# Third batch's output projection beside the sixteenth attention group instead of the fourteenth

## The chip, the cores and the metric

One core of one Trainium2 chip runs the whole kernel. The metric is the device time of one execution in microseconds (us); the engines are PE (TensorE, with PEld its weight loads), DVE (VectorE), ACT (ScalarE), POOL (GpSimd) and SP (SyncE, which here only issues DMAs).

## The reference

A gated cross-attention block and a gated mixture-of-experts block, in float32. Cut to what matters:

```python
# x (4, 512, 512); ctx (4, 1601, 512); 16 heads of 32
q = rms_norm(linear(layernorm(x), q_w, q_b), norm_q_w)
k, v          = ... of ctx[:, 257:]     # 1344 text rows
k_img, v_img  = ... of ctx[:, :257]     # 257 image rows
out = attention(q, k, v) + attention(q, k_img, v_img)   # softmax(q k^T / sqrt(32)) v
x = x + tanh(g_xattn[0]) * linear(out, o_w, o_b)
x = x + tanh(g_ffn[0]) * ffn(layernorm(x))              # shared expert and the top 2 of 8 experts
```

## The kernel before

**Stages.** The program projects queries, keys and values and writes them to DRAM, then runs the attention, then the feed-forward part. The change lies in the attention, which ends about 1269 us into the span. Semaphores alone order the engines; each engine's program is written out by hand.

**Groups and steps.** The attention has 16 groups `G` of 4 heads of one batch: batch `b` is groups 4b to 4b+3 (counted from 0, so the fourteenth group is G=13 and the sixteenth G=15). A group has 13 steps `kt`, one for each 128 of the 1601 keys. In a step PE makes four score products (`score`, L954), ACT takes their exponentials into one of four `P` buffers (`exps`, L1079), PE multiplies an earlier step's `P` with the values (`weigh`, L909), and POOL adds the `P` of steps 1 to 7 into `sacc` (`add`, L1261); DVE adds that of step 8 (L1203), after which `sacc` is complete (`d_add`). The exponentials of step kt wait until step kt-4's `P` has been both weighed and added, so ACT runs at most four steps ahead of POOL. Scores go to three PSUM banks, so PE is at most three score products ahead of ACT.

**Work of the next group.** Beside its own steps, each group but the last makes 64 small products for the softmax maxima of the next group (`units`, L439 on PE, L632 on DVE), 7 of them in step 0. They need the next group's keys, whose DMAs SP issues at step 10 of the group before. G=15 has no such products.

**Results.** A group's result `oi` is split into a high part `aTh` (ACT, L1097) and a low part `aTl` (POOL, L1278), two groups later at step 1. When the four groups of a batch are there, `pe_project_tile` multiplies them with the output weight: 4 tiles of 12 matmuls (L49, L50, L51), one tile after the scores of steps 4, 6, 8 and 10 of groups 5, 9 and 13. `dve_project_tile` adds each tile to `acc` (L1136) and takes its mean and variance (L1138, L1140). The fourth batch's 4 tiles stand behind the last group, where DVE and ACT finish its result in quarters (L1233 to L1243, L1129).

**Also in the last group.** At steps 2, 5 and 8 SP loads the first feed-forward weights into dead value buffers (L894); at steps 4, 7 and 10 ACT rounds them (L1122) and DVE takes the rest (L1219). SP waits for the earlier piece before it issues the next one. Every group also clears a 2 MB piece of `Xg` by DMA (L896), as SP's step 5.

Of the kernel before, what the change touches and what calls it, by code (L numbers as in the profile page):

```python
# [6 lines left out]
F32 = mybir.dt.float32  # L7
F32R = mybir.dt.float32r
U32 = mybir.dt.uint32
ACT = mybir.ActivationFunctionType  # L10
ALU = mybir.AluOpType
AX = mybir.AxisListType

NB = 4
# [10 lines left out]
NG = 4 * NB  # L25
# [13 lines left out]
def program(nc, ap, ctx):  # L39
    pe, dve, act, pool, sp = nc.tensor, nc.vector, nc.scalar, nc.gpsimd, nc.sync  # L40
# [7 lines left out]
    def mm3(out, ah, al, bh, bl, first, last):  # L48
        pe.matmul(out, ah, bh, start=first, stop=False)  # L49
        pe.matmul(out, ah, bl, start=False, stop=False)  # L50
        return pe.matmul(out, al, bh, start=False, stop=last)  # L51
# [160 lines left out]
    def rows_ra(G):  # L212


        return 64 + 65 * G + 4 * sum(x < G for x in (5, 9, 13))

    def head_rows(d, G, c0, c1):
        return d[128 * (G % 4):128 * (G % 4) + 128, c0:c1].rearrange("(j p) s -> p j s", p=32)
# [619 lines left out]
    BANKS_RA = (0, 1, 5)  # L838
# [7 lines left out]
    def exp_no(G, kt, j):  # L846
        return 52 * G + 4 * kt + j + 1
# [12 lines left out]
    def sum_no(G, kt):  # L860
        return 7 * G + max(1, kt)

    def slot(G, kt):
        return (NKT * G + kt) % 4

# [6 lines left out]
    def sp_attend():  # L872
        all_projected(sp)
        sp.dma_start(wo[:], ap["o_wT"].rearrange("(k p) o -> p k o", p=128)).then_inc(s_wo, 16)
        load_queries(2)
        load_values(1)
        for step in range(NSTEP):
            G, kt = divmod(step, NKT)
            pG = G - 1
            if kt == 12 and G + 1 < NG:  # L880
                store_mrow(G + 1)
            if kt == 1 and G >= 1 and pG + 2 < NG:
                sp.wait_ge(p_pv, pv_no(pG, 12))
                load_values(pG + 2)
            for i in range(3):
                if step == LASTG + 2 + 3 * i:
                    if i == 0:
                        sp.wait_ge(p_pv, pv_no(NG - 2, 12))
                        sp.wait_ge(p_sc, exp_no(NG - 2, 12, 3))
                    else:  # L890
                        sp.wait_ge(a_early, i)
                        sp.wait_ge(d_early, i)
                    for q in range(2):
                        sp.dma_start(early[:, :, 256 * q:256 * q + 256], first_weights(2 * i, q)).then_inc(s_gu, 16)  # L894
            if kt == 5 and G < NG:
                sp.dma_start(Xg[1024 * G:1024 * G + 1024, :], ap["zeros"]).then_inc(s_zero, 16)  # L896
            if kt == 10 and G + 2 < NG:
                sp.wait_ge(p_sc, exp_no(G, 9, 3))
                load_keys(G + 2, 0)
            if kt == 12 and G + 2 < NG:  # L900
                sp.wait_ge(p_sc, exp_no(G, 12, 3))
                load_keys(G + 2, 1)
                if G + 3 < NG:
                    load_queries(G + 3)
# [4 lines left out]
            ins = pe.matmul(ps[32 * j:32 * j + 32, bank, :], w(j), pt[p0:p1_, j, :], start=first, stop=last, tile_position=(p0, 32 * j))  # L909
        return ins  # L910

    def pe_project_tile(t, bank):
        for kk in range(4):
            ins = mm3(ps[:, bank, :], aTh[:, kk, 128 * t:128 * t + 128], aTl[:, kk, 128 * t:128 * t + 128],
                      Woh[:, kk, :], Wol[:, kk, :], kk == 0, kk == 3)
        ins.then_inc(p_ra, 1)

    def pe_attend():
# [3 lines left out]
        def ra_bank():  # L922
            if ra >= 68:
                pe.wait_ge(d_ra, ra - 2)
            return BANKS_RA[(ra - 65) % 3]
# [67 lines left out]
        for step in range(NSTEP):  # L993
            G, kt = divmod(step, NKT)
            more = G + 1 < NG
            plan = PLAN[kt] if more else [0] * 7
            at = sum(map(sum, PLAN[:kt])) if more else 0
            upto = [at + sum(plan[:i]) for i in range(8)]

            def place(i):  # L1000
                units(G + 1, upto[i], plan[i])

            def scored(j):
                if G < NG:
                    score(G, kt, j)

            if kt == 0:
                place(0)
                place(1)
                if G:  # L1010
                    image(G - 1)
                place(2)
                for j in range(4):
                    scored(j)
                    place(3 + j)
                continue
            scored(0)
            place(0)
            scored(1)
            place(1)  # L1020
            if kt == 1 and G:
                image_end(G - 1)
            if kt == 3:
                weigh(G, 0, 0, 128, True, False)
            if 3 <= kt < 11:
                weigh(G, kt - 2, 0, 128, False, False)
            if kt == 11:
                text_end(G)
            if kt == 12:
                weigh(G, 10, 64, 128, True, False)  # L1030
                if more:
                    pe.wait_ge(d_mx, G + 2)
                    pe.wait_ge(d_ra, ra)
                    pe_mrow(BANKS_RA[(ra - 65) % 3])
                    ra += 1
            place(2)
            scored(2)
            place(3)
            scored(3)
            place(4)  # L1040
            place(5)
            place(6)
            if G in (5, 9, 13) and kt in (4, 6, 8, 10):
                if kt == 4:
                    pe.wait_ge(a_ath, G - 1)
                    pe.wait_ge(g_atl, G - 1)
                    if G == 5:
                        pe.wait_ge(g_wol, 4)
                pe_project_tile((kt - 4) // 2, ra_bank())
                ra += 1  # L1050
        for t in range(4):
            pe.wait_ge(a_ath, NG + t)
            pe.wait_ge(d_last, 7 * t + 7)
            pe_project_tile(t, ra_bank())
            ra += 1


# [5 lines left out]
    def act_attend():  # L1063
# [27 lines left out]
        def split(G):  # L1091
            if G == 0:
                act.wait_ge(g_wol, 4)
            act.wait_ge(g_oi, 2 * G + 2)
            if G >= 4 and G % 4 == 0:
                act.wait_ge(p_ra, rows_ra(G + 2) + 1)
            act.activation(aTh[:, G % 4, :], oi[:], ACT.Copy).then_inc(a_ath, 1)  # L1097

        for step in range(NSTEP):
            G, kt = divmod(step, NKT)  # L1100
# [25 lines left out]
        for t in range(4):  # L1126
            cs = slice(128 * t, 128 * t + 128)
            act.wait_ge(d_last, 7 * t + 6)
            act.activation(aTh[:, 3, cs], oi[:, cs], ACT.Copy).then_inc(a_ath, 1)  # L1129
        root_of_variance_act(NB - 1)  # L1130


    def dve_project_tile(b, t, ra, bank):
        k = 4 * b + t
        dve.wait_ge(p_ra, ra + 1)
        dve.scalar_tensor_tensor(acc[:, k, :], ps[:, bank, :], tg[:, 0:1], acc[:, k, :], ALU.mult, ALU.add).then_inc(d_ra, 1)  # L1136
        dve.wait_ge(d_ra, ra + 1)
        dve.bn_stats(st3[:, k, 0:6], acc[:, k, :]).then_inc(d_st3, 1)  # L1138
        dve.wait_ge(d_st3, 2 * k + 1)
        dve.bn_aggr(st3[:, k, 6:8], st3[:, k, 0:6]).then_inc(d_st3, 1)  # L1140
# [8 lines left out]
    def dve_attend():  # L1149
# [17 lines left out]
        for step in range(NSTEP):  # L1167
# [41 lines left out]
                reciprocals(pG, (2,))  # L1209
            else:  # L1210
                units(G + 1, at, sum(plan))
            if G in (5, 9, 13) and kt in (4, 6, 8, 10):
                dve_project_tile((G - 5) // 4, (kt - 4) // 2, ra, BANKS_RA[(ra - 65) % 3])
                ra += 1
            for i in range(3):
                if step == LASTG + 4 + 3 * i:
# [14 lines left out]
        for t in range(4):  # L1231
            cs = slice(128 * t, 128 * t + 128)
            dve.tensor_tensor(oi[:, cs], ps[:, 6, cs], rt[:, cs], ALU.mult).then_inc(d_last, 1)  # L1233
            dve.wait_ge(d_last, 7 * t + 1)
            dve.tensor_tensor(rt[:, cs], rt[:, cs], ps[:, 7, cs], ALU.mult).then_inc(d_last, 1)
            dve.tensor_tensor(ot[:, cs], ot[:, cs], ps[:, 7, cs], ALU.mult).then_inc(d_last, 1)
            dve.wait_ge(d_last, 7 * t + 3)
            dve.reciprocal(rt[:, cs], rt[:, cs]).then_inc(d_last, 1)
            dve.tensor_tensor(oi[:, cs], oi[:, cs], ot[:, cs], ALU.add).then_inc(d_last, 1)
            dve.wait_ge(d_last, 7 * t + 5)  # L1240
            dve.tensor_tensor(oi[:, cs], oi[:, cs], rt[:, cs], ALU.mult).then_inc(d_last, 1)
            dve.wait_ge(a_ath, NG + t)
            dve.tensor_tensor(aTl[:, 3, cs], oi[:, cs], aTh[:, 3, cs].bitcast(F32), ALU.subtract).then_inc(d_last, 1)  # L1243
            if t:
                dve_project_tile(NB - 1, t - 1, ra, BANKS_RA[(ra - 65) % 3])
                ra += 1
# [4 lines left out]
    def pool_attend():  # L1251
# [21 lines left out]

        def split(G):
            pool.wait_ge(a_ath, G + 1)
            if G >= 4 and G % 4 == 0:
                pool.wait_ge(p_ra, rows_ra(G + 2) + 1)
            pool.tensor_tensor(aTl[:, G % 4, :], oi[:], aTh[:, G % 4, :].bitcast(F32), ALU.subtract).then_inc(g_atl, 1)  # L1278

        for step in range(NSTEP):  # L1280
            G, kt = divmod(step, NKT)
# [838 lines left out]
```

## Time and profile before

| | |
|---|---|
| median of 3 runs | 1810.65 us (1809.1 to 1810.71) |
| profiled execution | 1810.86 us, its span 1809.5 us |
| busy share of the span | PE 96%, DVE 66%, POOL 52%, ACT 45% |
| a group that follows a plain group | 49.96 us (G=8, most of the others) |
| groups 5, 9 and 13, with tiles | 62.19, 62.27 and 64.88 us |

A group's length is read between two starts of the one ACT instruction L638 that each group has at its step 12 (for example at 1075.05 and 1139.93 us for G=13). In the profile, busy time of PE holds matmuls that overlap in the array, so that 96% does not say that it never waits; the granted clock (PEclk) is 1.00 at 2.4 GHz and 0.50 at 1.2 GHz.

### The profile page before, as it was taken

Reading aid. Unit: us, or ns where it says so; the run is one execution under the profiler, and the core shown is the slowest. Engines: PE = TensorE matmul, PEld = TensorE weight load, DVE = VectorE, ACT = ScalarE, POOL = GpSimd, SP = SyncE. Lnnn points to the kernel's source line nnn. Section 1 sums busy time; section 2 is a strip of 40 time slices with the busy share of each in tenths; the row PEclk is TensorE's granted clock in tenths of the full one; section 3 lists DMA queues with packets and bytes.
Section 4 is the critical chain, followed back from the end, with each engine's and each line's share of the span. In section 5 each row is a group of like instructions: output and inputs, shape, how many; then the busy total and the mean of one; then the engine's idle time right before and its main releaser. Section 6 shows DMA issues by size and latency. Waiting matters only on the chain. (4 is left out here: it accounts for less than half of the span.)

```text
span 1809.5 us, 24750 instructions
## 1 busy us (share of the span) xinstructions
PE 1737.9 (96%) x8822; PEld 1119.7 (62%) x8822; DVE 1190.3 (66%) x2242; ACT 820.1 (45%) x1519; POOL 940.5 (52%) x323
## 2 busy tenths in 40 slices
PE   5999999999999999999999999997899999999999
PEld 4888878874444445444444445433676778878777
DVE  5776777667887777888778777835555445443555
ACT  4443332336555554565556554563221265554221
POOL 3221311118776664777746667673242377776442
PEclk8999999999999999999999999998999999999999
DMA  9456759546544553454355433320221578887442
GB/s 315 124 173 200 228 173 231 173 149 165 136 116 118 138 138 66 122 133 124 108 138 138 115 92 89 102 71 12 97 104 49 174 227 262 272 277 230 147 121 93
DMA packets 185234, 268.73 MB, mean 149 GB/s; under 512 B 24956, under 2 KB 121996, under 8 KB 184596
## 3 DMA queue, kind: packets, MB, share of 16 engines
q1 hardware_dynamic: 179992, 250.36, 47.6%
q0 software_dynamic: 5120, 16.78, 2.7%
q8 instruction: 71, 1.16, 0.3%
q14 instruction: 51, 0.42, 0.1%
HBM read 194.10 MB, written 105.93 MB: 166 GB/s over the span
## 5 line engine op out<-in xcount | busy, mean ns | idle before, releaser
L1079 ACT ACTIVATE P<-ps 128x512 f32<-128x512 f32 (+1 forms) x832 | 442.6, 597 | 330.9 <-PE ps L954 276.0
L632 DVE TENSOR_REDUCE mp<-ps 128x1 f32<-128x448 f32 x768 | 428.2, 615 | 96.0 <-PE ps L439 95.4
L1261 POOL TENSOR_TENSOR sacc<-sacc,P 128x2048 f32<-128x2048 f32 x96 | 441.6, 4600 | 13.8
L439 PE MATMUL ps<-Kst,Qst 96*128 96x448 f32 (+1 forms) x1024 | 386.9, 392 | 12.1 <-DMA Kst<-KLd 6.2
L954 PE MATMUL ps<-Qst,Kst 100*128 100x512 f32 (+1 forms) x832 | 323.5, 409 | 10.4 <-ACT P L1079 10.0
L439 PEld LDWEIGHTS ps<-Kst,Qst 96*128 96x128 f32 x1024 | 191.6, 188 | 227.9 <-DVE mp L632 141.3
L909 PE MATMUL ps<-P,Vg 128*32 128x512 f32 (+2 forms) x1792 | 237.8, 612 | 0.0
L808 POOL TENSOR_TENSOR cl<-craw,ch 128x1024 fp32r<-128x1024 f32 (+2 forms) x26 | 61.9, 2380 | 288.3 <-ACT ch L544 288.3
L954 PEld LDWEIGHTS ps<-Qst,Kst 100*128 100x128 f32 (+1 forms) x832 | 152.7, 186 | 69.9 <-ACT P L1079 43.4
L49 PE MATMUL ps<-W,ch 128*128 128x512 f32 (+1 forms) x408 | 162.7, 399 | 0.0
L51 PE MATMUL ps<-W,cl 128*128 128x512 f32 (+1 forms) x408 | 159.7, 392 | 0.0
L50 PE MATMUL ps<-W,ch 128*128 128x512 f32 (+1 forms) x408 | 159.6, 391 | 0.0
L2019 POOL TENSOR_TENSOR gul<-gur,guh 128x2048 fp32r<-128x2048 f32 x15 | 69.4, 4629 | 115.5 <-ACT guh L1692 115.4
L632 DVE TENSOR_REDUCE mx<-ps 128x1 f32<-128x258 f32 x256 | 96.0, 420 | 30.9 <-PE ps L439 30.3
L1261 POOL TENSOR_TENSOR sacc<-P 128x2048 f32<-128x2048 f32 x16 | 73.3, 4583 | 63.8 <-ACT P L1079 38.6
L2019 POOL TENSOR_TENSOR Kst<-gur,Kst 128x2048 fp32r<-128x2048 f32 x15 | 69.4, 4626 | 44.5 <-ACT Kst L1692 44.5
L51 PEld LDWEIGHTS ps<-W,cl 128*128 128x128 f32 (+1 forms) x408 | 75.9, 186 | 17.9 <-issue 0.2
L49 PEld LDWEIGHTS ps<-W,ch 128*128 128x128 f32 (+1 forms) x408 | 76.2, 187 | 15.4 <-issue 0.2
L50 PEld LDWEIGHTS ps<-W,ch 128*128 128x128 f32 (+1 forms) x408 | 76.2, 187 | 15.3
L909 PEld LDWEIGHTS ps<-P,Vg 128*32 128x32 f32 (+2 forms) x1792 | 39.0, 108 | 72.9 <-issue 44.3
L909 PE MATMUL ps<-P,ones 64*32 64x512 f32 (+2 forms) x640 | 82.7, 602 | 0.0
L564 ACT ACTIVATE junk<-kf 128x512 f32<-128x512 f32 (+1 forms) x51 | 32.2, 631 | 108.6 <-DVE kf L680 108.6
(227 smaller groups left out, 3008.2 us busy)
## 6 DMA issues: line engine op xcount, KB each, us to landing
gur<-in_w_gate_up SPq DMA_DIRECT2D x23, 1024.0 KB, 8.1
Kst<-KHd SPq DMA_DIRECT2D x32, 640.0 KB, 8.1
Vd<-vf SPq DMA_DIRECT2D x50, 256.0 KB, 2.3
craw<-in_ctxT SPq DMA_DIRECT2D x24, 512.0 KB, 4.7
KHd<-sth SPq DMA_DIRECT2D x24, 512.0 KB, 3.5
KLd<-stl SPq DMA_DIRECT2D x24, 512.0 KB, 4.7
dnr<-in_w_down SPq DMA_DIRECT2D x23, 512.0 KB, 3.9
xg<-Xg SPq DMA_DIRECT2D x23, 512.0 KB, 8.2
```

Of the source, the lines that this page charges most:

```text
L49: pe.matmul(out, ah, bh, start=first, stop=False)
L50: pe.matmul(out, ah, bl, start=False, stop=False)
L51: return pe.matmul(out, al, bh, start=False, stop=last)
L439: pe.matmul(ps[:, bank, 0:c1 - c0], Qst[G % 3][0:96, j, 128 * qt:128 * qt + 128], Kst[G % 2][0:96, j, c0:c1], start=True, stop=True).then_ ...
L564: act.activation(junk[:rows], kf[:rows, u % 3, :], ACT.Square, accum_out=stk[:rows, u % 4, 0:1]).then_inc(a_sqk, 1)
L632: dve.reduce_max(out, ps[:, bank, 0:c1 - c0], AX.X).then_inc(d_ra, 1)
L808: pool.tensor_tensor(cl[:, n % 3, :, 0:c1 - c0], craw[:, n % 3, :, 0:c1 - c0], ch[:, n % 2, :, 0:c1 - c0].bitcast(F32), ALU.subtract).then ...
L909: ins = pe.matmul(ps[32 * j:32 * j + 32, bank, :], w(j), pt[p0:p1_, j, :], start=first, stop=last, tile_position=(p0, 32 * j))
L954: pe.matmul(ps[:m, 2 + (e - 1) % 3, :], Kst[s][0:100, j, 128 * kt:128 * kt + m], Qst[G % 3][0:100, j, :], start=True, stop=True).then_inc( ...
L1079: act.activation(P[slot(G, kt)][:m, j, :], ps[:m, 2 + (e - 1) % 3, :], ACT.Exp, scale=SCALE).then_inc(a_exp, 1)
L1261: pool.tensor_tensor(sacc[:], (P[slot(G, 0)] if kt == 1 else sacc)[:], P[slot(G, kt)][:], ALU.add).then_inc(g_sum, 1)
L2019: pool.tensor_tensor(gul[q % 2], gur[raw_slot(q)][:], guh[q % 2].bitcast(F32), ALU.subtract).then_inc(g_gu, 1)
```

## The change

The third batch's four tiles leave steps 4, 6, 8 and 10 of group 13 and stand at the same steps of group 15. Since `aTh` and `aTl` must then hold the third batch longer, the results of groups 12 to 15 go to the query buffers `Qst[1]` and `Qst[2]` once the last group that reads them is through (`a_high`, `a_low`). The waits follow. The clearing DMA of `Xg` moves from step 5 to step 2 in SP's program.

```diff
-        return 64 + 65 * G + 4 * sum(x < G for x in (5, 9, 13))
+        return 64 + 65 * G + 4 * sum(x < G for x in (5, 9))
...
+    PROJECTED = {5: 0, 9: 1, 15: 2}
+
+    def a_high(G):
+
+        return aTh[:, G % 4, :] if G < 12 else Qst[1 if G < 14 else 2][:, 2 * (G % 2), :]
+
+    def a_low(G):
+        return aTl[:, G % 4, :] if G < 12 else Qst[1 if G < 14 else 2][:, 2 * (G % 2) + 1, :]
...
-            if kt == 5 and G < NG:
+            if kt == 2 and G < NG:
                 sp.dma_start(Xg[1024 * G:1024 * G + 1024, :], ap["zeros"]).then_inc(s_zero, 16)
...
-            if G in (5, 9, 13) and kt in (4, 6, 8, 10):
+            if G in PROJECTED and kt in (4, 6, 8, 10):
+                b = PROJECTED[G]
                 if kt == 4:
-                    pe.wait_ge(a_ath, G - 1)
-                    pe.wait_ge(g_atl, G - 1)
-                    if G == 5:
+                    pe.wait_ge(a_ath, 4 * b + 4)
+                    pe.wait_ge(g_atl, 4 * b + 4)
+                    if b == 0:
                         pe.wait_ge(g_wol, 4)
-                pe_project_tile((kt - 4) // 2, ra_bank())
+                pe_project_tile(b, (kt - 4) // 2, ra_bank())
                 ra += 1
...
-            if G >= 4 and G % 4 == 0:
+            if G in (4, 8):
                 act.wait_ge(p_ra, rows_ra(G + 2) + 1)
-            act.activation(aTh[:, G % 4, :], oi[:], ACT.Copy).then_inc(a_ath, 1)
+            if G >= 12:
+                act.wait_ge(p_sc, exp_no(13 if G < 14 else 14, 12, 3))
+            act.activation(a_high(G), oi[:], ACT.Copy).then_inc(a_ath, 1)
...
-            if G in (5, 9, 13) and kt in (4, 6, 8, 10):
-                dve_project_tile((G - 5) // 4, (kt - 4) // 2, ra, BANKS_RA[(ra - 65) % 3])
+            if G in PROJECTED and kt in (4, 6, 8, 10):
+                dve_project_tile(PROJECTED[G], (kt - 4) // 2, ra, BANKS_RA[(ra - 65) % 3])
                 ra += 1
```

POOL's `split` and the last four tiles change in the same way. Line numbers in the order of the change are higher by 9 to 16 than those of the profile (L954 is L964 there, L909 L919, L1136 L1149, L1219 L1232, L1165 L1178, L1203 L1216).

PE, last group, from step 9's late scores to the start of step 11's end; before:

```order
L954 MATMUL ps<-Qst,Kst 128x512 x4
L909 MATMUL ps<-P,Vg 32x512 x4
L954 MATMUL ps<-Qst,Kst 128x512 x4
L909 MATMUL ps<-P,Vg 32x512 x8
L909 MATMUL ps<-P,ones 32x512 x8
L954 MATMUL ps<-Qst,Kst 128x512 x2
```

PE, the same place in the change:

```order
L964 MATMUL ps<-Qst,Kst 128x512 x4
L919 MATMUL ps<-P,Vg 32x512 x4
L964 MATMUL ps<-Qst,Kst 128x512 x2
L49 MATMUL ps<-Woh,aTh 128x512
L50 MATMUL ps<-Wol,aTh 128x512
L51 MATMUL ps<-Woh,aTl 128x512
...
L964 MATMUL ps<-Qst,Kst 128x512 x2
L919 MATMUL ps<-P,Vg 32x512 x8
L919 MATMUL ps<-P,ones 32x512 x8
L964 MATMUL ps<-Qst,Kst 128x512 x2
```

The fourth tile (12 matmuls, of which three are shown) now stands between step 10's last score and step 11's first, ahead of the eight value products and eight row sums that close the text part.

DVE, last group, from the third early weight to the end of the `sacc` sum; before:

```order
L1219 TENSOR_TENSOR Kst<-Vg,Kst 128x1024 x3
L1165 RECIPROCAL rt<-rt 128x128
L1203 TENSOR_TENSOR sacc<-sacc,P 128x2048
L1165 RECIPROCAL rt<-rt 128x128 x3
```

DVE, the same place in the change:

```order
L1149 SCALAR_TENSOR_TENSOR acc<-ps,tg,acc 128x512
L1151 BN_STATS st<-acc 128x6
L1153 BN_AGGR st<-st 128x2
L1232 TENSOR_TENSOR Kst<-Vg,Kst 128x1024
L1178 RECIPROCAL rt<-rt 128x128
L1216 TENSOR_TENSOR sacc<-sacc,P 128x2048
L1178 RECIPROCAL rt<-rt 128x128 x3
```

The three instructions of the fourth tile, which wait for PE's tile, stand ahead of the third early weight and of the addition that completes `sacc`.

SP, from the last group's two row copies on; before:

```order
L321 DMA Qst<-mrh 2x4x512
L321 DMA Qst<-mrl 2x4x512
L894 DMA Vg<-in_w_sh_gate_up 128x2x256 x4
L896 DMA Xg<-in_zeros 32x16384
L894 DMA Vg<-in_w_sh_down 128x2x256 x2
```

SP, the same place in the change:

```order
L321 DMA Qst<-mrh 2x4x512
L321 DMA Qst<-mrl 2x4x512
L904 DMA Vg<-in_w_sh_gate_up 128x2x256 x2
L906 DMA Xg<-in_zeros 32x16384
L904 DMA Vg<-in_w_sh_gate_up 128x2x256 x2
L904 DMA Vg<-in_w_sh_down 128x2x256 x2
```

Only here does the clearing DMA pass anything: it now goes out behind the first early weight instead of behind the second. In the groups before, it follows the value loads either way.

## Rows read from the trace of the kernel before

**Rows 1.** Windows of six groups: length; busy PE, PEld, DVE, ACT, POOL; PEclk; DMA.

```profile
548.61:601.35 52.74, 50.72 (x281) 23.08 (x280) 40.47 (x74) 29.61 (x56) 35.89 (x10) 0.97 0.45 118
651.74:713.93 62.19, 61.33 (x329) 31.64 (x328) 46.13 (x86) 29.90 (x56) 35.97 (x10) 1.00 0.40 101
713.93:763.28 49.35, 48.83 (x281) 22.93 (x280) 40.32 (x74) 29.59 (x56) 35.96 (x10) 1.00 0.50 126
813.24:863.20 49.96, 49.07 (x281) 22.84 (x280) 40.30 (x74) 29.65 (x56) 35.90 (x10) 1.00 0.49 125
1075.05:1139.93 64.88, 62.87 (x329) 31.82 (x328) 46.29 (x86) 29.90 (x56) 35.97 (x10) 0.97 0.38 96
1139.93:1189.53 49.60, 49.10 (x281) 22.72 (x280) 40.30 (x74) 29.64 (x56) 35.92 (x10) 1.00 0.23 71
```

**Rows 2.** PE's timeline where groups 3 and 13 begin: start, length, instruction, [idle before].

```profile
550.54 0.68 PE L439 MATMUL ps<-Kst,Qst 96*128 96x448 f32 x2 [1.51 <-DMA Kst<-KLd]
...
1076.84 0.84 PE L439 MATMUL ps<-Kst,Qst 96*128 96x448 f32 x2 [1.36 <-DMA Kst<-KLd]
```

**Rows 3.** Windows of 5 us: start of group 13, and two in group 15.

```profile
1075.00:1080.00 5.00, 3.63 (x17) 0.90 (x18) 3.55 (x5) 1.93 (x4) 0.49 (x1) 0.72 0.18 39
...
1209.00:1214.00 5.00, 4.78 (x24) 1.74 (x24) 1.44 (x1) 4.23 (x9) 4.86 (x2) 1.00 0.45 144
...
1219.00:1224.00 5.00, 3.46 (x11) 1.07 (x11) 1.89 (x1) 2.08 (x4) 4.86 (x2) 0.66 0.38 121
```

**Rows 4.** PE's timeline, group 13: first matmul of its fourth tile, and the next score.

```profile
1129.12 0.50 PE L49 MATMUL ps<-Woh,aTh 128*128 128x512 f32 x1
...
1131.97 0.40 PE L954 MATMUL ps<-Qst,Kst 100*128 100x512 f32 x1
```

**Rows 5.** POOL's timeline, group 15: its additions of steps 1 to 7.

```profile
1200.32 4.57 POOL L1261 TENSOR_TENSOR sacc<-P 128x2048 f32<-128x2048 f32 x1 [1.68 <-ACT P L1079]
1205.03 29.62 POOL L1261 TENSOR_TENSOR sacc<-sacc,P 128x2048 f32<-128x2048 f32 x6
```

**Rows 6.** ACT's timeline, group 15: exponentials of steps 10, 11, and 11 with 12.

```profile
1230.06 2.08 ACT L1079 ACTIVATE P<-ps 128x512 f32<-128x512 f32 x4 [2.62 <-POOL sacc L1261]
...
1234.74 1.09 ACT L1079 ACTIVATE P<-ps 128x512 f32<-128x512 f32 x2 [1.66 <-PE ps L909]
...
1237.78 2.13 ACT L1079 ACTIVATE P<-ps 128x512 f32<-128x512 f32 x4 [1.47 <-PE ps L954]
```

**Rows 7.** PE's timeline, group 15: late scores of steps 8, 10 and 11.

```profile
1220.54 1.77 PE L954 MATMUL ps<-Qst,Kst 100*128 100x512 f32 x3 [1.79 <-ACT P L1079]
...
1230.71 1.77 PE L954 MATMUL ps<-Qst,Kst 100*128 100x512 f32 x3 [0.60 <-ACT P L1079]
1232.41 2.92 PE L909 MATMUL ps<-P,Vg 128*32 128x512 f32 x16
...
1237.24 0.95 PE L954 MATMUL ps<-Qst,Kst 100*128 100x512 f32 x3
```

**Rows 8.** DVE's timeline, group 15: third early weight, and the sum into `sacc`.

```profile
1233.11 2.62 DVE L1219 TENSOR_TENSOR Kst<-Vg,Kst 128x1024 fp32r<-128x1024 f32 x1 [12.23 <-ACT Kst L1122]
...
1236.52 2.22 DVE L1203 TENSOR_TENSOR sacc<-sacc,P 128x2048 f32<-128x2048 f32 x1
```

**Rows 9.** Line L1219's three instructions: shortest, median and longest ns.

```profile
L1219 DVE TENSOR_TENSOR Kst<-Vg,Kst x3: 1437/2625/2651, 1209.2 to 1233.1; 128x1024 fp32r<-128x1024 f32 x3
```

**Rows 10.** Timelines behind group 15: first tile of the fourth batch on PE, then DVE.

```profile
1249.81 0.76 PE L49 MATMUL ps<-Woh,aTh 128*128 128x512 f32 x1 [3.78 <-ACT aTh L1129]
...
1254.90 0.40 PE L49 MATMUL ps<-Woh,aTh 128*128 128x512 f32 x1
...
1255.10 0.75 DVE L1136 SCALAR_TENSOR_TENSOR acc<-ps,tg,acc 128x512 f32<-128x512 f32 x1 [2.54 <-PE ps L51]
...
1256.71 0.26 DVE L1233 TENSOR_TENSOR oi<-ps,rt 128x128 f32<-128x128 f32 x1
```

**Rows 11.** SP's timeline in group 15: the clearing DMA.

```profile
1211.69 0.61 SPq L896 DMA_DIRECT2D Xg<-in_zeros  x1
```

More of the change, by code:

```diff
@@ L910, in pe_heads, with pe_project_tile @@
         return ins
-    def pe_project_tile(t, bank):
+    def pe_project_tile(b, t, bank):
         for kk in range(4):
-            ins = mm3(ps[:, bank, :], aTh[:, kk, 128 * t:128 * t + 128], aTl[:, kk, 128 * t:128 * t + 128],
+            ins = mm3(ps[:, bank, :], a_high(4 * b + kk)[:, 128 * t:128 * t + 128], a_low(4 * b + kk)[:, 128 * t:128 * t + 128],
                       Woh[:, kk, :], Wol[:, kk, :], kk == 0, kk == 3)
@@ L1053, in pe_attend @@
             pe.wait_ge(d_last, 7 * t + 7)
-            pe_project_tile(t, ra_bank())
+            pe_project_tile(NB - 1, t, ra_bank())
             ra += 1
@@ L1128, in act_attend @@
             act.wait_ge(d_last, 7 * t + 6)
-            act.activation(aTh[:, 3, cs], oi[:, cs], ACT.Copy).then_inc(a_ath, 1)
+            act.activation(a_high(NG - 1)[:, cs], oi[:, cs], ACT.Copy).then_inc(a_ath, 1)
         root_of_variance_act(NB - 1)
@@ L1242, in dve_attend @@
             dve.wait_ge(a_ath, NG + t)
-            dve.tensor_tensor(aTl[:, 3, cs], oi[:, cs], aTh[:, 3, cs].bitcast(F32), ALU.subtract).then_inc(d_last, 1)
+            dve.tensor_tensor(a_low(NG - 1)[:, cs], oi[:, cs], a_high(NG - 1)[:, cs].bitcast(F32), ALU.subtract).then_inc(d_last, 1)
             if t:
@@ L1275, in split @@
             pool.wait_ge(a_ath, G + 1)
-            if G >= 4 and G % 4 == 0:
+            if G in (4, 8):
                 pool.wait_ge(p_ra, rows_ra(G + 2) + 1)
-            pool.tensor_tensor(aTl[:, G % 4, :], oi[:], aTh[:, G % 4, :].bitcast(F32), ALU.subtract).then_inc(g_atl, 1)
+            if G >= 12:
+                pool.wait_ge(p_sc, exp_no(13 if G < 14 else 14, 12, 3))
+            pool.tensor_tensor(a_low(G), oi[:], a_high(G).bitcast(F32), ALU.subtract).then_inc(g_atl, 1)
         for step in range(NSTEP):
```

## The prediction

> **What bounds the kernel now.** I read the windows of the groups first. PE sets the pace of the groups that also make the next group's products. A group without tiles takes 49.96 us; groups 5 and 13, which hold a batch's four tiles, take 62.19 and 64.88 us [rows 1]. POOL's and ACT's busy time is the same in both kinds (35.9 to 36.0 and 29.6 to 29.9 us), so what is added is PE's, and every tile lengthens the attention.
>
> Group 15 has no such products, and there the timelines of POOL, ACT and PE show another bound. POOL adds without a break from 1200.32 to 1234.65 us, seven additions [rows 5]; ACT's exponentials of steps 10 and 11 start when an addition ends, four steps behind (1230.06 and, behind POOL's end at 1234.65, 1234.74) [rows 6]. PE waits for ACT: 1.79 us ahead of 1220.54, 0.60 us ahead of 1230.71 [rows 7], with matmuls that themselves run slowly, since the granted clock is 0.66 in 1219 to 1224 against 1.00 in 1209 to 1214 [rows 3]. So the tiles leave a place where PE is the bound for one where it mostly waits. The question is how much of them sticks out at the end of group 15.
>
> **What leaves group 13.** Four tiles of 12 matmuls. The last of them takes 1131.97 - 1129.12 = 2.85 us until the next score [rows 4], so four take 11.4 us of PE. The whole cost is better read from the groups: 62.19 - 49.96 = 12.2 us for group 5, and I take that. Group 13's own 64.88 holds 2.6 us more. That is another matter: at its start PE waited 1.36 us for keys, and the clock then fell to 0.72 [rows 2, 3]. Group 3, which has no tiles, did the same (1.51 us of waiting, 52.74 us instead of 49.96) [rows 1, 2]. All this lies ahead of the first tile, so nothing in the change touches it: group 13 should take 52.6 us. If this dip should be absent, 2.6 us more are won; that is a bound.
>
> **What that does to group 14.** A group behind one with tiles is shorter (49.35 and 49.60 us against 49.96) [rows 1]: the tile of step 10 gave the next keys 2.85 us more to land. Now group 14 follows a plain group, and I charge 49.96 - 49.35 = 0.6 us. The bounds are 0 and, if it waits for its keys as groups 3 and 13 did, 2.8 us (52.74 - 49.96).
>
> **What enters group 15.** The tiles of steps 4, 6 and 8: PE's own work in a step there is four scores and a product of values, some 2 us at full clock (a tile's matmul takes 2.85/12 = 0.24 us, so four scores take 1.0, and I count as much for the values), against 29.62/6 = 4.94 us from one POOL addition to the next [rows 5]. Two steps leave 9.9 - 4 = 5.9 us for a tile of 2.85. ACT is delayed by each tile but runs ahead of POOL: the step-7 addition starts near 1229.7 (1234.65 - 4.94), while its exponentials are due by step 8's first late score at 1220.54 [rows 5, 7], 9 us earlier. I cost these three tiles at nothing, hidden under POOL's additions; without that cover they would cost up to 8.6 us.
>
> The tile of step 10 has no such cover. It can't start before step 10's last score, which waits for an exponential that itself waits for POOL (1230.71) [rows 7], so it starts near 1231.1. Behind it on PE are step 11's first two scores and the 16 products and sums that close the text part, and then step 11's late scores (1237.24) [rows 7]; behind it on DVE are the third early weight and the addition that completes `sacc` [rows 8], on which step 12's exponentials, the image sums and POOL's normalising wait, so all of the end.
>
> What the tile takes depends on the clock. Step 9's exponentials start one addition ahead of step 10's, near 1230.06 - 4.9 = 1225.2 [rows 5, 6]; PE follows them with about 2 us of work that each of them releases in turn, done by about 1228.3 (an estimate), and waits until 1230.7, some 2.4 us. Waits of 1.79 us and of 1.36 us left it at half clock for the matmuls behind them [rows 2, 3, 7], so I take half clock. The row that shows such a tile is the fourth batch's first, behind a wait of 3.78 us: 1254.90 - 1249.81 = 5.1 us on PE, and 5.3 us until DVE starts on it [rows 10]. The sum on DVE: 1231.1 + 5.3 = 1236.4; the tile's three instructions take 1256.71 - 1255.10 = 1.6 us [rows 10], to 1238.0; the early weight, shortest 1.44 us, longest 2.65 [rows 9], to 1239.4. Before, it ended at 1233.11 + 2.62 = 1235.7 [rows 8]. So the `sacc` sum is **3.7 us** late. Both durations occur; I take the short one, since at this time POOL's additions, over which the last one lay, are over. With 2.62 it is 4.9.
>
> By the Trainium skill (GPSIMD Engine Reference, Specifications), GpSimd shares its SBUF interfaces with VectorE and the two contend when a VectorE instruction has two SBUF inputs, as this early weight has. The row of the last one, 2.62 us, lies partly over POOL's seventh addition, and so agrees; but one of the three took 1.44 us. By the rule the sum is 3.7, by the row of that very instruction 4.9.
>
> On PE the same place gives less: 1231.1 + 5.1 = 1236.2, two scores to 1236.7, then 4.0 us for the closing products (4.8 before, from 1232.41 to 1237.24, which began at half clock), to 1240.7, which is 3.4 us late [rows 7]. The two delays run side by side, and the later counts: 3.7 us. At full clock it would be 1231.0 + 2.85 + 0.2 + 1.6 + 1.44 = 1237.1 on DVE, 1.4 us late, and 1.1 us on PE. Bounds: 1.4 and 4.9.
>
> **The rest.** The waits of the new buffers are for group 13's or 14's last scores, which lie well ahead of the splits that follow two groups later; the same copies write elsewhere: nothing. The clearing DMA moves only in group 15, from 1211.69 [rows 11] to about 1199; nothing there waits for it, it leaves the second early weight's way, and the early weights keep at least 2 us of slack: nothing. Behind the attention all is the same work, shifted.
>
> **Sum.** -12.2 + 0.6 + 3.7 = -7.9 us. The profiled execution took 1810.86 us, 0.2 above the median, so the working holds for the median: 1810.65 - 7.9 = 1802.75, or **1802.7 us**.
>
> **The rivals.**
>
> Full clock in the last tile. PE is busier in group 15 than before, and the clock may hold. For: it held until 1219 with short waits [rows 3]. Against: the long wait ahead of step 10's last score stays. Time: 1810.65 - 12.2 + 0.6 + 1.4 = 1800.5. Chance 0.27.
>
> The keys of group 15 come late. The tile of step 10 no longer covers their landing, PE waits some 1.4 us at group 14's start and loses clock: 2.8 in place of 0.6. For: two groups did this [rows 1, 2]; against: group 8, behind a plain group too, did not. Time: 1810.65 - 12.2 + 2.8 + 3.7 = 1805.0. Chance 0.14.
>
> Slower than before. PE falls to half clock early in group 15 and becomes its bound. Then a step costs four scores and a product at twice the time, 4 us, and a tile 5.1: steps 4 to 10 take 7 x 4 + 4 x 5.1 = 48 us from 1205 on, to 1253, where PE was before at 1232.4 [rows 7]. That is 21 us against 11.6 won (12.2 - 0.6): 1810.65 + 9.4 = 1820. It decides once over 11.6 us stick out of group 15, more than half of it at half clock. Against: full clock where the first tiles are to stand [rows 3], and denser work there than before. Chance 0.03.
>
> The gain is lost elsewhere: three tiles not hidden, or group 13 held by another engine. Against the latter: groups 6 and 8 run at 49.4 to 50.0 with the same POOL and ACT work [rows 1]. With all three tiles exposed: 1802.7 + 8.6 = 1811.3, no change. Chance 0.06.
>
> The likeliest case has 0.50. The range of the likeliest case and the first two rivals, with the bounds of 1.4 and 4.9, reaches from 1798 (full clock, part of the absent dip) to 1806.5 (late keys and the slow early weight): 1810.65 - 12.2 + 2.8 + 4.9 = 1806.2. About 0.2% (3.6 us) is what a measurement of this kernel can tell from no change; faster by more has 0.91, no change 0.06, slower 0.03.
>
> **What would show it.** Right: group 13 at 52.6 us (or 50 without the dip), group 14 near 50.2; in group 15 POOL's seven additions still unbroken and ending within 1 us of 1234.65 - 12.2 + 0.6 = 1223.0; the last tile at about 0.43 us a matmul; the `sacc` sum some 3.7 us later against POOL's last addition than its present 1236.52 against 1234.65. Wrong: a gap among POOL's additions (an early tile sticks out), a tile at 0.24 us a matmul, or an early weight in front of which DVE waits for ACT or a DMA. What would break the forecast most is PE at half clock before step 8.

## The result, and the profile after

The change takes 1801.4 us (median of 8 runs, 1798.17 to 1803.67) against 1810.21 us before (8 runs, 1805.7 to 1812.19): ratio 0.9954, 95% interval 0.9942 to 0.9965. It is faster by 8.8 us; 7.9 were forecast. The profiled execution's span is 1801.2 us against 1809.5, 8.3 less.

The windows of the change for group 13, 14, 15 (up to DVE's first instruction on the fourth batch's result) and for the feed-forward part; columns as in [rows 1]:

```profile
1075.76:1127.01 51.25, 49.13 (x281) 22.85 (x280) 40.48 (x74) 29.68 (x57) 35.90 (x10) 1.00 0.47 122
1127.01:1177.43 50.42, 49.26 (x281) 22.62 (x280) 40.31 (x74) 29.63 (x56) 35.93 (x10) 1.00 0.22 70
1177.43:1235.91 58.48, 54.84 (x310) 22.34 (x308) 25.59 (x32) 36.15 (x67) 40.10 (x12) 1.00 0.19 64
1258.56:1801.20 542.64, 522.48 (x2402) 414.05 (x2402) 264.87 (x501) 192.25 (x283) 275.46 (x124) 0.99 0.52 171
```

The same two last stretches of the kernel before, which [rows 1] does not hold:

```profile
1189.53:1246.78 57.25, 50.25 (x262) 14.50 (x260) 17.12 (x21) 35.77 (x67) 39.87 (x12) 0.91 0.19 65
1269.59:1809.50 539.91, 520.50 (x2402) 412.91 (x2402) 264.45 (x501) 192.09 (x283) 275.64 (x124) 0.99 0.53 172
```

The reader is to see four things. Group 13 is 13.6 us shorter, group 14 0.8 us longer, and group 15, with 48 matmuls more (310 against 262), only 1.2 us longer: together 11.6 us won. The granted clock over group 15 is 1.00 instead of 0.91. And the feed-forward part, the same code in both, is 2.7 us longer in the change's trace, which hides part of the gain; the rest of the difference to 8.3 is mainly 0.7 us ahead of group 13, in code that is the same in both as well.

PE's timeline around the last tile in group 15 of the change, to be laid beside [rows 7]:

```profile
1217.30 0.51 PE L964 MATMUL ps<-Qst,Kst 100*128 100x512 f32 x1
1218.76 0.50 PE L964 MATMUL ps<-Qst,Kst 100*128 100x512 f32 x1 [0.95 <-ACT P L1090]
1219.10 0.40 PE L49 MATMUL ps<-Woh,aTh 128*128 128x512 f32 x1
...
1221.85 0.63 PE L964 MATMUL ps<-Qst,Kst 100*128 100x512 f32 x2
1222.41 2.06 PE L919 MATMUL ps<-P,Vg 128*32 128x512 f32 x16
...
1226.38 0.95 PE L964 MATMUL ps<-Qst,Kst 100*128 100x512 f32 x3
```

PE waits 0.95 us ahead of step 10's last score, not 2.4, and the tile takes 1221.85 - 1219.10 = 2.75 us: full clock, 0.23 us a matmul.

POOL's and DVE's timelines there, beside [rows 5] and [rows 8]:

```profile
1188.20 4.58 POOL L1274 TENSOR_TENSOR sacc<-P 128x2048 f32<-128x2048 f32 x1 [1.67 <-ACT P L1090]
1192.92 29.85 POOL L1274 TENSOR_TENSOR sacc<-sacc,P 128x2048 f32<-128x2048 f32 x6
...
1222.05 0.75 DVE L1149 SCALAR_TENSOR_TENSOR acc<-ps,tg,acc 128x512 f32<-128x512 f32 x1 [6.83 <-PE ps L51]
...
1223.66 1.19 DVE L1232 TENSOR_TENSOR Kst<-Vg,Kst 128x1024 fp32r<-128x1024 f32 x1
1224.77 0.94 DVE L1178 RECIPROCAL rt<-rt 128x128 f32<-128x128 f32 x1
1225.63 2.23 DVE L1216 TENSOR_TENSOR sacc<-sacc,P 128x2048 f32<-128x2048 f32 x1
```

POOL's seven additions have no gap (they end at 1222.77, 45.3 us into the group against 45.1 before), so the three early tiles are covered: their work on PE lies under POOL's additions and delays none of them. The sum into `sacc` starts 2.9 us behind POOL's end; before it was 1236.52 - 1234.65 = 1.9. That is 1.0 us, and the additions' 0.2 us more make the 1.2.

### The profile page after: what moved, and what is told of

It reads as the page before. It is cut to its first block and busy times, and to the rows that moved or that the text cites. A ratio compares the mean times of both kernels' runs of the same rounds, so it can differ in the third digit from the quotient of the medians.

```text
span 1801.2 us, 24754 instructions
## 1 busy us (share of the span) xinstructions
PE 1728.6 (96%) x8822; PEld 1117.5 (62%) x8822; DVE 1193.7 (66%) x2242; ACT 820.6 (46%) x1519; POOL 940.5 (52%) x323
## 5 line engine op out<-in xcount | busy, mean ns | idle before, releaser
L964 PE MATMUL ps<-Qst,Kst 100*128 100x512 f32 (+1 forms) x832 | 320.0, 405 | 6.3 <-ACT P L1090 6.0
L919 PE MATMUL ps<-P,Vg 128*32 128x512 f32 (+2 forms) x1792 | 235.4, 606 | 0.0
L964 PEld LDWEIGHTS ps<-Qst,Kst 100*128 100x128 f32 (+1 forms) x832 | 151.8, 185 | 61.1 <-ACT P L1090 38.7
L919 PEld LDWEIGHTS ps<-P,Vg 128*32 128x32 f32 (+2 forms) x1792 | 38.7, 108 | 71.4 <-issue 46.4
L919 PE MATMUL ps<-P,ones 64*32 64x512 f32 (+2 forms) x640 | 82.5, 601 | 0.0
```

Of the source, the lines that this page charges most:

```text
L964: pe.matmul(ps[:m, 2 + (e - 1) % 3, :], Kst[s][0:100, j, 128 * kt:128 * kt + m], Qst[G % 3][0:100, j, :], start=True, stop=True).then_inc( ...
```

## The experiments

Twelve experiments, of which r9 to r12 repeat kernels that had run already. Each has one trace, from which the table is read (us); the lengths are between the starts of L638, group 15's up to DVE's first instruction on the fourth batch's result. The times of the kernel before and of the change are medians of 8 runs, those of r6, r7, r10, r11 and r12 of 5 or 6, the others single runs.

| kernel | G=13 | G=14 | G=15 | feed-forward | time |
|---|---|---|---|---|---|
| before | 64.88 | 49.60 | 57.25 | 539.91 | 1810.21 |
| change | 51.25 | 50.42 | 58.48 | 542.64 | 1801.4 |
| r1 clearing early | 64.99 | 49.57 | 57.24 | 542.73 | one run, 1813.9 |
| r2 tiles back | 64.98 | 49.55 | 63.75 | 543.05 | one run, 1819.81 |
| r3 all tiles light | 50.99 | 50.58 | 61.95 | 542.15 | one run, 1800.67 |
| r4 early tiles light | 52.84 | 50.49 | 58.33 | 542.12 | one run, 1798.55 |
| r5 DVE's part behind | 51.08 | 50.49 | 58.49 | 545.01 | one run, 1803.9 |
| r6 steps 3, 4, 6, 8 | 52.61 | 50.50 | 57.27 | 544.20 | 1801.71 |
| r7 and DVE adds step 7 | 52.61 | 50.75 | 60.84 | 541.53 | 1801.43 |
| r8 steps 9 to 12 | 52.56 | 50.62 | 66.46 | 544.98 | one run, 1811.1 |
| r9 before again | 65.07 | 49.54 | 57.60 | 543.40 | one run, 1814.35 |
| r10 change again | 51.05 | 50.43 | 58.54 | 543.07 | 1801.54 |
| r11 steps 3, 4, 6, 8 again | 51.14 | 50.62 | 57.27 | 541.84 | 1798.49 |
| r12 as r7, again | 51.07 | 50.37 | 60.85 | 545.17 | 1799.49 |

**r1: the clearing DMA alone**

```diff
 # the kernel before
-            if kt == 5 and G < NG:
+            if kt == 2 and G < NG:
```

> The kernel before with the clearing DMA moved to step 2 and nothing else. My theory: it moves only in group 15, where nothing waits for it. Groups 13, 14 and 15 as before (64.9 or 62.2, 49.6, and 57.3 us from L638's last start to the first instruction of the fourth batch's result on DVE). Rival (the early weights land sooner and take some of the change's gain): group 15 shorter by 0.5 us or more.

Groups 13 to 15 are as before to 0.1 us. The clearing DMA's place is worth nothing in them, as expected. The feed-forward part takes 542.73 us, not 539.91:

```profile
1189.76:1247.00 57.24, 50.28 (x262) 14.38 (x260) 17.12 (x21) 35.72 (x67) 39.87 (x12) 0.91 0.19 65
1269.87:1812.60 542.73, 522.13 (x2402) 414.00 (x2402) 261.60 (x501) 191.80 (x283) 275.84 (x124) 0.99 0.51 171
```

In the fourteen traces the feed-forward part takes 541.5 to 545.2 us but once, and that once, 539.91, is the trace from which I forecast. The kernel before alone gives 539.91 and, in r9, 543.40. So the 2.7 us are within what the same code varies by, and nothing here shows that the change lengthens this part.

**r2: tiles back in group 13, all else as in the change**

```diff
 # the change
-        return 64 + 65 * G + 4 * sum(x < G for x in (5, 9))
+        return 64 + 65 * G + 4 * sum(x < G for x in (5, 9, 13))
-    PROJECTED = {5: 0, 9: 1, 15: 2}
+    PROJECTED = {5: 0, 9: 1, 13: 2}
```

> The change with its new buffers, waits and early clearing DMA, but the third batch's tiles back in group 13. My theory: all of the gain is the tiles' place, so this one takes what the kernel before takes, group 13 at 62 to 65 us and group 15 at 57.3. Rival (buffers or waits matter): total or group 14 or 15 off by over 1 us.

Groups 13 and 14 return to 64.98 and 49.55: the gain there is the tiles' place and nothing else. Group 15 is a surprise, 63.75, and so is the total, 1819.81 us in one run; both are off by more than the 1 us that the rival named. Of the 9.0 us by which this trace's span is longer than that of the kernel before, 6.5 are group 15's and 3.1 the feed-forward part's. Group 15's window, and 10 us of it from 45 us on, where the closing products stand:

```profile
1188.72:1252.47 63.75, 57.16 (x262) 15.85 (x260) 22.02 (x20) 35.85 (x67) 39.81 (x12) 0.79 0.17 59
...
1233.72:1243.72 10.00, 10.00 (x44) 1.71 (x36) 8.17 (x7) 4.03 (x8) 4.55 (x3) 0.50 0.00 0
```

The same instructions of group 15 as before, but PE at half clock over the whole end. That is where 4.6 us of the 6.5 more come from; the other 1.9 come from an earlier stretch at half clock, some 7.5 to 17.5 us into the group, which puts POOL's first addition 12.7 us in instead of 10.8. The buffers by themselves cost at most some 0.2 us: with them and full clock (the change) POOL's additions stand where they stood. Whether they make that early stretch likelier is not shown. It came in four of the eleven traces with the new buffers (r2, r7, r8, r12) and in none of the three without (before, r1, r9), which is too few to tell.

**r3: the third batch's tiles cut to one matmul each**

```diff
 # the change, in pe_project_tile
+        if b == 2 and t in (0, 1, 2, 3):
+            ins = pe.matmul(ps[:, bank, :], a_high(4 * b)[:, 128 * t:128 * t + 128], Woh[:, 0, :], start=True, stop=True)
-        for kk in range(4):
+        for kk in range(0 if b == 2 and t in (0, 1, 2, 3) else 4):
```

> The change with each of the third batch's four tiles cut from 12 matmuls to 1 (the projection of batch 3 is left out but for one product); DVE's part stays. If POOL's additions cover PE's part of the tiles but the last, and the last tile's DVE part ahead of the sum into sacc is what sticks out, group 15 takes 57.5 to 58.5 us, at most 1 us less than the change's 58.5. If PE's part of the tiles is what lengthens it, it falls to 57.3 or below.

Neither outcome that I had named came: 61.95 us, more than with the work left in. The windows of group 15, and of 10 us of it from 45 us on, with the closing products in them:

```profile
1172.31:1234.26 61.95, 56.83 (x266) 15.82 (x264) 29.25 (x32) 35.68 (x67) 39.86 (x12) 0.81 0.17 60
...
1217.31:1227.31 10.00, 10.00 (x42) 2.00 (x38) 6.73 (x7) 4.24 (x9) 2.67 (x3) 0.50 0.00 0
```

Up to the sum into `sacc` this kernel is as the kernel before, 47.0 us into the group in both; with the tile's PE work the change has 48.2. Then the closing products run at half clock, and the group ends 4.7 us later than in the kernel before. So in this one trace 44 matmuls less went with a group 3.5 us longer than the change's. That leaving them out always costs this is not shown: the kernel before, with no tile in the group at all, took 57.25 and 57.60. What all traces show is where the clock holds. In the seven whose four tiles stand whole at steps 3 to 10 (the change, r5, r6, r7, r10, r11, r12) it is 1.00 from 18 us into group 15 to its end; in each of the other seven it falls to 0.50 at least once there.

**r4: only the early tiles light**

The same edit with `t in (0, 1, 2)`.

> The change with the tiles of steps 4, 6 and 8 cut to 1 matmul each (most of the projection of three quarters of batch 3 is left out), the tile of step 10 whole. The forecast had PE wait 2.4 us ahead of that tile and run it at half clock; in the change it waited 0.95 us at full clock. My theory now: it was the tile of step 8 that filled this wait. Then here PE waits 1.5 us or more, the granted clock falls, the last tile takes about 5.1 us and group 15 takes 60 to 61 us, longer than with the work left in. Rival (the clock holds in this kernel for another reason): full clock, a tile of 2.85 us and 58.5 us or less.

PE's timeline ahead of the last tile:

```profile
1204.85 0.50 PE L966 MATMUL ps<-Qst,Kst 100*128 100x512 f32 x1 [1.80 <-ACT P L1092]
...
1210.33 1.77 PE L966 MATMUL ps<-Qst,Kst 100*128 100x512 f32 x3 [2.58 <-ACT P L1092]
1212.04 1.94 PE L919 MATMUL ps<-P,Vg 128*32 128x512 f32 x8
1213.90 0.50 PE L966 MATMUL ps<-Qst,Kst 100*128 100x512 f32 x1
1215.02 0.50 PE L966 MATMUL ps<-Qst,Kst 100*128 100x512 f32 x1 [0.61 <-ACT P L1092]
1215.36 0.39 PE L49 MATMUL ps<-Woh,aTh 128*128 128x512 f32 x1
```

Half of my theory holds. Without the early tiles PE waits again, 1.80 and 2.58 us, and the eight value products behind the second wait take 1.94 us instead of 1.06. But the slow stretch is over before the tile, which runs at 0.23 us a matmul, and the slow products fill the time so that only 0.61 us of waiting is left ahead of step 10's last score. Group 15 takes 58.33 against the change's 58.48 and 58.54: the three early tiles cost some 0.2 us. No trace shows the whole tile at half clock that the forecast's 3.7 us stood for; r8 comes nearest.

**r5: DVE's part of the last tile behind the sum**

```diff
 # the change, in dve_attend
-            if G in PROJECTED and kt in (4, 6, 8, 10):
-                dve_project_tile(PROJECTED[G], (kt - 4) // 2, ra, BANKS_RA[(ra - 65) % 3])
+            if G in PROJECTED and kt in ((4, 6, 8, 10) if G < 15 else (4, 6, 8, 11)):
+                dve_project_tile(PROJECTED[G], min(3, (kt - 4) // 2), ra, BANKS_RA[(ra - 65) % 3])
```

> The change with DVE's three instructions of the last tile moved behind the sum that completes sacc (from step 10 to step 11 of group 15); PE's order is as in the change. If what sticks out of group 15 is DVE's order, the sum starts within 0.3 us of its place relative to POOL's last addition in the kernel before (1.9 us behind its end) and group 15 takes 57.3 to 57.6 us. If it is PE's order (the closing products behind the tile), it stays near 58.3 to 58.5.

The sum starts early again, and nothing comes of it. DVE's and ACT's timelines:

```profile
1223.39 2.22 DVE L1216 TENSOR_TENSOR sacc<-sacc,P 128x2048 f32<-128x2048 f32 x1
...
1225.70 2.05 ACT L1090 ACTIVATE P<-ps 128x512 f32<-128x512 f32 x4 [1.79 <-PE ps L964]
```

The group starts at 1176.22. The sum stands 47.2 us into it (change 48.2, before 47.0), but ACT's exponentials of step 11's late scores wait for PE and start at 49.5, as in the change (1226.92 - 1177.43), against 48.25 before ([rows 6], 1237.78 - 1189.53). Group 15 takes 58.49. So the tile's place on PE, ahead of the closing products, costs the 1.2 us by itself, and DVE's order adds nothing to it here.

**r6 and r11: tiles one to two steps earlier**

```diff
 # the change; the same on DVE
+    def tile_steps(G):
+        return (4, 6, 8, 10) if G < 15 else (3, 4, 6, 8)
-            if G in PROJECTED and kt in (4, 6, 8, 10):
+            if G in PROJECTED and kt in tile_steps(G):
```

> The change with group 15's tiles at steps 3, 4, 6 and 8 instead of 4, 6, 8 and 10. My theory: POOL's additions cover all four, so group 15 takes 57.3 to 57.6 us and the kernel is some 1 us faster than the change (1800.4 against 1801.4). Rival: PE then waits 2 us ahead of step 10's last score, falls to half clock behind it and closes the text part slowly, as before the change (group 15 at 57.3 all the same), or the tile of step 3 delays ACT until POOL has a gap (58 or more).

> Tiles of group 15 at steps 3, 4, 6 and 8, once more. My theory: group 15 takes 57.3 us again and the last tile is off the path. Rival: as for the change, 58.5.

57.27 us in both traces, the 1.2 us are gone, and the clock holds:

```profile
1175.46:1232.73 57.27, 54.62 (x310) 22.34 (x308) 21.75 (x32) 36.20 (x67) 40.14 (x12) 1.00 0.19 66
```

So in these two traces the third batch's projection is free: group 15 takes what it took without it. On one chip, beside the change, this kernel takes 1798.49 us (5 runs, 1797.81 to 1800.55) against 1801.54 (6 runs, 1800.31 to 1806.54); the ratios to the kernel before there are 0.9926 (0.9912 to 0.994) and 0.9949 (0.9934 to 0.9964). It beats the kernel before; against the change its median is 3 us lower, with one pair of times that overlaps (1800.55 and 1800.31). Of these 3 us the traces explain 1.2. On another chip r6 took 1801.71 us, where the kernel before took 1815.35 (0.9929, 0.9903 to 0.9955).

**r8: tiles where little covers them**

The same edit with `(9, 10, 11, 12)`.

> The change with group 15's tiles at steps 9, 10, 11 and 12, where little of POOL's additions is left to cover them. If the cover is what makes the early tiles free, two more of 2.85 us stick out, and group 15 takes 58.5 + 5.7 = 64 us, or up to 67 with slow matmuls. Rival (PE has room there as well, between the exponentials): under 61 us.

66.46 us, 8.0 more than the change, of which 1.6 are the early stretch at half clock (POOL's first addition at 12.3 us instead of 10.8). About 6.4 us are left for the tiles' place, against 5.7 expected: what made the early tiles free is POOL's chain. PE's timeline at the tile of step 9:

```profile
1213.60 0.50 PE L967 MATMUL ps<-Qst,Kst 100*128 100x512 f32 x1 [1.75 <-ACT P L1093]
1213.93 0.40 PE L49 MATMUL ps<-Woh,aTh 128*128 128x512 f32 x1
...
1218.27 0.63 PE L967 MATMUL ps<-Qst,Kst 100*128 100x512 f32 x2
```

Behind a wait of 1.75 us this tile takes 1218.27 - 1213.93 = 4.34 us, where the change's last takes 2.75; most of its matmuls run at half clock. That is the slow tile of the forecast, in another place; up to 1.6 of the 6.4 us may be its.

**r9 and r10: both kernels again**

> The kernel before, once more, for its trace. Without tiles in group 15 PE waits there again and again; my theory: where the half-clock stretches fall differs from run to run, so group 15 takes 57.3 us when they end ahead of the closing products and 60 us or more when one lies on them, as in the kernel with the tiles back in group 13 (63.8). Groups 1 to 14 and the feed-forward part differ by up to 3 us each from the first trace without any change. Rival: this kernel repeats 57.3 us and the clock's stretches to 0.1.

> The change once more, beside the one with tiles at steps 3, 4, 6 and 8. My theory: group 15 again at full clock to its end and 58.5 us, the kernel some 1 us slower than with the tiles one to two steps earlier, which the spread of single times (some 6 us) may hide. Rival (the full clock was chance): a stretch at half clock in the second half of group 15, and 60 us or more.

```profile
1189.09:1246.69 57.60, 51.34 (x262) 14.75 (x260) 17.12 (x20) 35.74 (x67) 39.87 (x12) 0.88 0.19 65
```

The kernel before repeats group 15 within 0.35 us, at 57.60, but not its slow stretches (clock 0.88 instead of 0.91). So neither my theory nor the rival of r9 holds whole: the stretches do move from execution to execution, and here that cost next to nothing. Group 3 takes 51.02 us instead of 52.74, the feed-forward part 543.40 instead of 539.91. The change repeats 58.54 at full clock, in another execution:

```profile
1174.83:1233.37 58.54, 54.84 (x310) 22.34 (x308) 25.63 (x33) 36.13 (x67) 40.11 (x12) 1.00 0.18 64
```

**r7 and r12: DVE adds step 7**

```diff
 # as r6
-            if G < NG and 2 <= kt < 9:
+            if G < NG and 2 <= kt < (9 if G < NG - 1 else 8):
                 add(G, kt - 1)
 # in dve_attend, ahead of the early weights
+            if step == LASTG + 9:
+                dve.wait_ge(a_exp, exp_no(G, 7, 3))
+                dve.wait_ge(g_sum, sum_no(G, 6))
+                dve.tensor_tensor(sacc[:], sacc[:], P[slot(G, 7)][:], ALU.add).then_inc(g_sum, 1)
```

> As the one with tiles at steps 3, 4, 6 and 8, and DVE instead of POOL adds step 7 in group 15. If POOL's chain of seven additions is what bounds group 15, taking one of 4.7 us out and putting 2.3 us on DVE shortens it by about 2 us, to 55 to 55.5 us, and the kernel to about 1798.5. Rival (PE or ACT is the bound there once the tiles are in): no change against 57.5.

> Tiles of group 15 at steps 3, 4, 6 and 8, and step 7 added by DVE instead of POOL, once more, since the first run fell to half clock ahead of the tiles. With full clock there: POOL's six additions end near 40.6 us into the group, DVE's addition of step 7 near 43, against POOL's 45.4, the sum into sacc starts near 45 instead of 47.2, and group 15 takes 55.3 us against 57.3, the kernel some 2 us less than 1798.5. Rival (ACT or PE sets the end of the group once the tiles are in): 57 us or more.

Inconclusive. In both traces the clock fell to half some 7.5 us into group 15; r12's windows of the group, and of 10 us of it from 10 us on:

```profile
1177.42:1238.27 60.85, 58.40 (x310) 23.55 (x308) 28.99 (x34) 36.18 (x67) 34.69 (x11) 0.92 0.18 62
...
1187.42:1197.42 10.00, 10.00 (x36) 4.49 (x33) 1.29 (x2) 5.22 (x10) 7.45 (x2) 0.61 0.73 260
```

In them PE is the bound, as the forecast's slower rival had it: POOL's six additions end 41.4 us in, but PE starts the last tile only at 38.8 (35.2 in r6) and from 20 us in waits no more than 0.22 us at a time. The group takes 60.85, 3.6 more than r6. DVE's part of the plan did not come about either: its addition of step 7 starts at 44.05, 2.6 us behind POOL's end, because the second early weight (4.58 us) and the last tile stood ahead of it. r12's profiled execution was its slowest (1807.68 us, the other five 1796.18 to 1802.07), and no trace shows this kernel without the early stretch. The medians show no gain: r7's 1801.43 us is close to r6's 1801.71 on the same chip, and r12's 1799.49 is of another chip than r11's 1798.49. Whether the kernel gains 2 us at full clock stays open.

## Why the prediction was right, and where it was off

**The bound.** Right. Group 13 lost its tiles' time; r2 puts it back and gets 64.98.

**What leaves group 13: 12.2 us.** Measured 13.6. I took group 13's dip (2.6 us, a stretch at half clock near its start) to be untouched, and gave it whole to the changed kernel, 52.6 us. Ten traces without tiles in group 13 fall in two: six at 51.0 to 51.3 with the clock at 1.00 (the change among them), and four at 52.6 to 52.8 with 0.97; four with tiles lie at 64.9 to 65.1. PE's timeline of the change where groups 13 and 14 begin:

```profile
1077.80 0.67 PE L439 MATMUL ps<-Kst,Qst 96*128 96x448 f32 x2 [1.62 <-DMA Kst<-KLd]
...
1128.07 0.67 PE L439 MATMUL ps<-Kst,Qst 96*128 96x448 f32 x2 [0.64 <-DMA Kst<-KLd]
```

PE waited longer for group 13's keys than in [rows 2], 1.62 us against 1.36, so the wait stayed, but the clock over the group is 1.00: the slow stretch behind the wait did not come. The wait is there in all fourteen traces (1.4 to 1.6 us), and the stretch behind it in eight, with the same work on PE up to that point. So the forecast's 12.2 is what the tiles are worth (64.98 - 52.6 = 12.4 where the dip is in both), and the other 1.4 us of the 13.6 are the luck of this trace. The prediction named the absent dip, as a bound.

**Group 14: 0.6 us.** Measured 0.8; 0.8 to 1.2 in all traces. PE waits 0.64 us for keys at its start in the row above, and 0.6 to 0.9 in the others; where the tiles stand in group 13, this wait is absent. The late-keys rival didn't occur in any of the ten traces without tiles in group 13.

**The early tiles: nothing.** Right: 0.2 us by r4, no gap on POOL, and 6.4 us more when the tiles stand where the cover ends (r8).

**The last tile: 3.7 us.** Measured 1.2; this is the step that failed. "And waits until 1230.7, some 2.4 us", from which half clock followed, left out that the tile of step 8 fills that wait: with it PE is a little late for step 9, and the wait is 0.95 us. That half clock follows a wait was itself too sure: behind 1.75 us it came in r8, behind group 13's 1.4 to 1.6 us in eight traces of fourteen. The first rival, full clock with 1.4 us, is what happened, in the change, in r5 and in r10. I weighed it at 0.27; the busier PE was the stronger argument. The sum on DVE was right in form (tile to DVE, 1.6 us, weight, reciprocal, sum), but PE's side is worth the same 1.2 us (1.1 forecast), and r5 shows that PE's side alone is enough for it.

**The early weight: 1.44 us, not 2.62.** Measured 1.19, behind POOL's last addition. The rule that I drew on, contention of GpSimd and VectorE on shared SBUF interfaces (the Trainium skill, GPSIMD Engine Reference, Specifications), is borne out, in a stronger form than I used. The 1.44 us that I held against it is no exception: alone the instruction takes 1.19, and that one too ended 0.94 us behind the start of a POOL addition, like the longer ones; see the last section.

**The sum.** Terms as measured: -13.6 + 0.8 + 1.2 = -11.6 us, against -7.9. The medians differ by 8.8 on the first comparison and by 11.2 on r10's (1812.77 to 1801.54); single times of one kernel spread over 3 to 12 us. So the comparisons themselves give anything from 9 to 11 us, and that the total came out within 1 us of the forecast is in part luck: the last tile was charged 2.5 us too much, and the absent dip gave 1.4 more.

**The slower rival.** It is real as a mechanism: in r2, r7, r8 and r12 the clock falls some 7.5 us into group 15, and in r7 and r12 PE with the tiles becomes the bound. Its price there is 3.6 us, not 21, a late start of 1.7 us among them, since the stretch ended after about 10 us. I gave it 0.03; the fall at the start came in four traces of fourteen, but without lasting.

## What to carry to other kernels

Work of the bounding engine is free where that engine waits in a stretch with another bound, but only as long as it still has waits behind that work in which to catch up: three tiles cost 0.2 us, the one right ahead of the closing products 1.2, and two steps earlier it too cost nothing. Fill waits of PE when you can: in the seven traces with whole tiles at steps 3 to 10 the clock held through the second half of group 15, in the seven others it fell, and in two of these (r2, r3) that cost over 4 us. Compare the parts of a kernel by windows between fixed instructions before you trust a total: here the part with identical code moved by up to 5 us.

## What the runs showed of the hardware

**A DVE instruction with two SBUF inputs waits for the end of POOL's.** In the change the first two early weights take 3.65 and 4.09 us, the third, behind POOL's last addition, 1.19. DVE's rows, and POOL's, as pairs of additions:

```profile
1199.67 3.65 DVE L1232 TENSOR_TENSOR Kst<-Vg,Kst 128x1024 fp32r<-128x1024 f32 x1
...
1209.52 4.09 DVE L1232 TENSOR_TENSOR Kst<-Vg,Kst 128x1024 fp32r<-128x1024 f32 x1 [2.26 <-ACT Kst L1135]
```

```profile
1197.66 10.12 POOL L1274 TENSOR_TENSOR sacc<-sacc,P 128x2048 f32<-128x2048 f32 x2
...
1202.38 10.15 POOL L1274 TENSOR_TENSOR sacc<-sacc,P 128x2048 f32<-128x2048 f32 x2
...
1207.93 4.60 POOL L1274 TENSOR_TENSOR sacc<-sacc,P 128x2048 f32<-128x2048 f32 x1
...
1212.67 10.10 POOL L1274 TENSOR_TENSOR sacc<-sacc,P 128x2048 f32<-128x2048 f32 x2
```

Additions start at 1202.38 and 1212.67. The early weights end at 1203.32 and 1213.61, 0.94 us behind these starts each time, whenever they began, and the addition that starts there takes some 5.4 us (the next one starts at 1207.93) instead of 4.6 (the one at 1207.93). So it reads as if the DVE instruction stands still while POOL's runs, gets its 1.1 us at the change-over, and POOL pays 0.8. The three of the kernel before fit: two ended 0.94 us behind the start of an addition, and that of 1233.11 ended at 1235.73, 1.1 us behind POOL's end [rows 8, 5]. So do all the others that met an addition, in all fourteen traces: 0.93 to 0.95 us behind a start, or 1.07 to 1.09 behind the last end. Two such additions stand in POOL's chain of seven, before and after the change, and 1.6 us of the bound of group 15 is theirs (an estimate, 2 x 0.8); early weights at another place were not tried. DVE's other instructions on a tile (one input in PSUM, or one input alone) keep 0.75 and 0.69 us beside POOL. That the DVE instruction is stopped, rather than slowed, is read from these ends and not tried by itself.

**Half clock is not always behind a wait that one sees.** In r2, r7, r8 and r12 the clock fell some 7.5 us into group 15, with waits of PE of 0.3 us as in the ten other traces, and stayed at 0.50 for about 10 us. In kernels that leave PE waiting in the second half of group 15 it lay at 0.50 over nearly all of the closing products twice (r2, r3). In before, r1, r4 and r9 it was back ahead of them or in their first 3 us, and the group took 57.2 to 58.3. What decides between them stays open.
